# Cross-attention on one core: low parts of the small half by transfer, context scales in one call, once-a-batch steps earlier in VectorE's queue

## The reference

```
xn = layernorm(ctx)            # ctx: 8 x 1601 x 192, gain and bias
ln = layernorm(layernorm(x))   # the latents, 64 a batch
q  = ln @ Wq.T
k, v = split(concat([xn @ Wkv.T, ln @ Wlkv.T], axis=1))
q, k = rmsnorm(q) * gain, rmsnorm(k) * gain        # per head of 64
attn = softmax(where(mask, q @ k.T / sqrt(64), -max))
x = x + (attn @ v) @ Wo.T + bo
```

## Time and profile before

| what | value |
|---|---|
| median of 3 runs | 519.65 us (518.51 to 521.28) |
| the profiled execution's own time | 514.96 us |
| its span, first to last instruction | 513.2 us |
| mean granted TensorE clock | 0.967 |
| TensorE busy | 427.2 us (83%) |
| VectorE busy | 402.1 us (78%) |
| GpSimd busy | 244.7 us (48%) |
| ScalarE busy | 239.1 us (47%) |

### The profile page before, as it was taken

How to read it: one execution, slowest core, us unless ns; L and a number is a source line. 1 busy time by engine, 2 the same in 40 slices (tenths; PEclk the granted TensorE clock), 3 DMA queues, 4 the chain that set the end, 5 groups by cost and what they waited for, 6 DMA issues and landing times.

```text
span 513.2 us, 6607 instructions
## 1 busy us (share of the span) xinstructions
PE 427.2 (83%) x2042; PEld 332.5 (65%) x2042; DVE 402.1 (78%) x969; ACT 239.1 (47%) x547; POOL 244.7 (48%) x248
## 2 busy tenths in 40 slices
PE   3786758788889878978989969887997789789996
PEld 0363535567767766867767758764374667568885
DVE  5846789999999999999988896425569556887776
ACT  0237744556575656755556535321242115335551
POOL 6351866658458465584575542001521331445550
PEclk9998978989999999999999999899999986999999
DMA  8604932040141131403100002910000000000001
GB/s 247 186 1 138 251 129 66 2 142 2 52 142 52 26 119 52 140 4 121 29 3 1 2 0 79 406 40 0 0 2 0 1 0 0 1 1 1 0 2 42
DMA packets 23975, 31.80 MB, mean 62 GB/s; under 512 B 2954, under 2 KB 19652, under 8 KB 23940
## 3 DMA queue, kind: packets, MB, share of 16 engines
q1 hardware_dynamic: 23940, 31.38, 19.8%
HBM read 30.69 MB, written 0.52 MB: 61 GB/s over the span
## 4 chain that ended last, share of the span: by engine, by line
DVE 42%; PE 29%; POOL 15%; issue 10%; ACT 2%; DMA 1%; SPq 1%; DVEq 0%; POOLq 0%; ACTq 0%
PE bank L571 27%; POOL kr L481 10%; DVE kss L1406 6%; DVE arena L1418 5%; DVE arena L1454 5%; DVE split_b L1397 5%; DVE cst L1343 3%; DVE arena L1613 2%; POOL crs L447 2%; DVE arena L1627 1%; DVE kguard L1409 1%; DVE big L1328 1%; DVE cmv L1347 1%; DMA mask_in<-in_p_mask 1%; DVE split_b L1687 1%
## 5 line engine op out<-in xcount | busy, mean ns | idle before, releaser
L571 PE MATMUL bank<-keyq,split_b 128*128 128x512 f32 (+2 forms) x724 | 168.4, 380 | 21.4 <-DVE split_b L1687 7.5
L571 PEld LDWEIGHTS bank<-keyq,split_b 128*128 128x128 f32 (+1 forms) x724 | 123.0, 192 | 52.3 <-issue 19.0
L481 POOL TENSOR_TENSOR kr<-kguard,neg_half 128x8 f32<-128x8 f32 (+1 forms) x56 | 93.3, 1666 | 104.6 <-DVE kguard L1409 104.4
L571 PE MATMUL bank<-arena 128*128 128x193 f32 (+4 forms) x528 | 100.0, 332 | 8.4 <-DVE arena L1613 4.4
L571 PEld LDWEIGHTS bank<-arena 128*128 128x128 f32 (+2 forms) x528 | 85.6, 192 | 18.2 <-issue 13.0
L1130 ACT ACTIVATE arena<-bank 128x512 f32<-128x512 f32 (+1 forms) x56 | 31.6, 563 | 73.4 <-PE bank L571 72.8
L571 PE MATMUL bank<-split_b,keyq 128*128 128x512 f32 x204 | 51.8, 405 | 0.0
L1397 DVE TENSOR_TENSOR split_b<-arena,split_b 32x256 fp32r<-32x256 f32 (+1 forms) x112 | 47.5, 424 | 2.5
L1418 DVE TENSOR_TENSOR arena<-bank,kr 128x512 f32<-128x512 f32 (+1 forms) x56 | 36.0, 643 | 15.3 <-POOL kr L481 15.1
L571 PEld LDWEIGHTS bank<-split_b,keyq 128*128 128x128 f32 x204 | 39.1, 197 | 7.7
L470 POOL TENSOR_TENSOR split_b<-arena,split_b 128x256 fp32r<-128x256 f32 (+1 forms) x56 | 38.4, 685 | 8.9 <-ACT split_b L1105 8.8
(11 more groups left out here) (221 smaller groups left out, 613.5 us busy)
## 6 DMA issues: line engine op xcount, KB each, us to landing
arena<-in_ctx SPq DMA_DIRECT2D x16, 576.0 KB, 4.2
arena<-in_p_ctxT SPq DMA_DIRECT2D x8, 800.5 KB, 6.4
arena<-in_p_ctxT SPq DMA_DIRECT2D x8, 400.2 KB, 7.1
arena<-in_p_experts SPq DMA_DIRECT2D x1, 2688.0 KB, 18.4
arena<-in_p_experts SPq DMA_DIRECT2D x1, 2304.0 KB, 12.1
arena<-in_p_experts SPq DMA_DIRECT2D x1, 1536.0 KB, 6.5
X<-in_x SPq DMA_DIRECT2D x1, 512.0 KB, 3.7
arena<-in_t_Wlkv SPq DMA_DIRECT2D x1, 512.0 KB, 6.9
```

The costliest lines, as they stand in the source:

```text
L481: pool.tensor_tensor(kr[0:r, n % 2, 0:k], kg_[0:r, n % 2, 0:k], neg_half[0:r, 0:4 * k].rearrange("p (t h) -> p t h", h=H), ALU.pow).then_i ...
L571: return nc.tensor.matmul(out_, l, r, start=start, stop=stop, skip_group_check=shared)
```

## The change

It does four things. First, `split_side` goes from VectorE. GpSimd subtracts all 64 small channels in one instruction, as a second part of `split_rest`, into a new tile `side_low` with two slots, and SyncE moves the result to partitions 96 to 127 of `xs` with two transfers of 32 partitions per group (`move_side`). TensorE waits for the transfers in place of the subtraction, and GpSimd, before it writes a slot again, for the transfers out of it. Second, SyncE's loop runs over groups: the moves of group `u + 2` stand first at each step, the loads are placed at steps 0, 1, 2 and 4 of a batch, the mixer's weights go out one a step from step 14 on. Third, GpSimd computes the context scales of a batch in one call with 13 columns at g 2. Fourth, VectorE does `evac_latent_out` ahead of the sums and `refold_low_part` right behind them, and ScalarE copies refolded keys (`twin`) at g 1 in place of g 0. The title of the change also names the scaling of the scores in the step of their sums; `norm_scores(u)` stands in the step of `key_sums(u)` before and after.

```diff
+        side_low = sb("side_low", [SMALL, 2, 256], F32R)
...
+            def move_side(n):
+                k = 256 if n % NG < NG - 1 else TAIL
+                sp.wait_ge(xs_side, n + 1)
+                for j in range(2):
+                    sp.dma_start(xs[n % 3][96:P, 2 + j, 0:k].bitcast(F32), side_low[32 * j:32 * j + 32, n % 2, 0:k].bitcast(F32)).then_inc(side_in[n % 3], 16)
...
+            move_side(0)
+            move_side(1)
+            for u in range(groups):
+                b, g = divmod(u, NG)
+                if u + 2 < groups:
+                    move_side(u + 2)
+                if g == 0 and b + 2 < B:
...
                     load_context(b + 2, 0)
+                if g in (1, 2) and b + 1 < B:
+                    load_turned(b + 1, g - 1)
+                if g == 4 and b + 1 < B:
+                    spread_sd(b + 1)
+                if g == 4 and b + 2 < B:
                     if b + 2 >= 4:
                         sp.wait_ge(y_part, NG * (b - 1))
                     load_context(b + 2, 1)
+                if 2 * NG <= u < 2 * NG + len(mixer_weights):
+                    dst, src = mixer_weights[u - 2 * NG]
+                    sp.dma_start(dst, src).then_inc(mixer_in, 16)
...
-            def context_scales(b, part):
+            def context_scales(b):
+                pool.wait_ge(caggr, 2 * b + 2)
                 k = b % 2
+                then(pool.tensor_scalar(cve[:, k], cmv[:, k, :, 1], LN_EPS, None, ALU.add))
+                then(pool.tensor_tensor(crs[:, k], cve[:, k], neg_half[:, 0:FULL + 1], ALU.pow))
+                if b:
                     pool.wait_ge(sdT_mm, b)
+                pool.tensor_tensor(csd[:], cve[:, k], crs[:, k], ALU.mult).then_inc(ctx_ready, 2)
...
                 pool.tensor_tensor(v[:, 1, 0:k], raw[:, 0], v[:, 0, 0:k].bitcast(F32), ALU.subtract).then_inc(xs_rest, 1)
+                pool.wait_ge(xs_small, n + 1)
+                if n >= 2:
+                    pool.wait_ge(side_in[(n - 2) % 3], 32 * ((n - 2) // 3 + 1))
+                pool.tensor_tensor(side_low[:, n % 2, 0:k], raw[0:SMALL, 1], v[0:SMALL, 2, 0:k].bitcast(F32), ALU.subtract).then_inc(xs_side, 1)
...
                 if g == 2 and b + 1 < B:
-                    context_scales(b + 1, 1)
+                    context_scales(b + 1)
...
-                if g == 0 and b + 1 < B:
-                    context_scales(b + 1, 0)
...
-                pe.wait_ge(xs_side, n + 1)
+                pe.wait_ge(side_in[n % 3], 32 * (n // 3 + 1))
...
+                if g == 1 and 2 <= b <= 5:
+                    act.wait_ge(refold_high, b - 1)
+                    twin((b + 2) % 4 + 1, (b + 2) % 4 + 2)
...
+                if g == 4 and 2 <= b <= B + 1:
+                    evac_latent_out(b - 2)
                 if u < groups:
                     key_sums(u)
+                if g == 0 and 2 <= b <= 5:
+                    refold_low_part(b + 2)
                 if g == 3 and 2 <= b <= B + 1:
                     evac_sum(b - 2)
-                if g == 4 and 2 <= b <= B + 1:
-                    evac_latent_out(b - 2)
...
-                if u + 2 < groups:
-                    split_side(u + 2)
...
-                if g == 0 and 2 <= b <= 5:
-                    refold_low_part(b + 2)
```

More of the change, by code:

```diff
@@ L236, in build @@
         sdT_mm = sem("sdT_mm"); sdT_evac = sem("sdT_evac")
-        sd_rest = sem("sd_rest"); xs_split = sem("xs_split"); xs_rest = sem("xs_rest"); xs_small = sem("xs_small"); xs_side = sem("xs_side")
+        sd_rest = sem("sd_rest"); xs_split = sem("xs_split"); xs_rest = sem("xs_rest"); xs_small = sem("xs_small"); xs_side = sem("xs_side"); side_in = [sem(f"side_in{i}") for i in range(3)]
         k_mm = sem("k_mm"); k_sq = sem("k_sq"); k_ss = sem("k_ss"); k_r = sem("k_r"); s_norm = sem("s_norm"); s_max = sem("s_max")
@@ L349, in _ @@
             sp.wait_ge(pool_const, 1)
-            load_turned(0)
+            mixer_weights = (
+                    (wo[:], a["t_Wo"].rearrange("(c p) n -> p c n", p=P)),
+                    (bo[:], a["L0_xattn_bo"].rearrange("(o d) -> o d", o=1)),
+                    (sums[:], a["c_sums"]), (pick[:], a["c_pick"]), (headsel[:], a["c_head"]),
+                    (wx0[:], a["t_W_x0"].rearrange("(c p) n -> p c n", p=P)),
+                    (wx2b[:], a["t_W_x2"][P:160, :]),
+                    (wr[:], a["t_W_r"].rearrange("(c p) n -> p c n", p=P)),
+                    (wk[:], a["t_W_k"].rearrange("(c p) n -> p c n", p=P)),
+                    (ww1[:], a["t_W_w1"].rearrange("(c p) n -> p c n", p=P)),
+                    (ww2[0:64, :], a["t_W_w2"]), (ww2[64:65, :], a["L0_attn_b_w2"].rearrange("(o d) -> o d", o=1)),
+                    (wv[:], a["t_W_v"].rearrange("(c p) n -> p c n", p=P)),
+                    (wg[:], a["t_W_g"].rearrange("(c p) n -> p c n", p=P)),
+                    (wo2[:], a["t_W_o"].rearrange("(c p) n -> p c n", p=P)),
+                    (gatew[:], a["t_gate_w"].rearrange("(c p) n -> p c n", p=P)),
+                    (ebias[:], a["L0_ffn_e_bias"].rearrange("(o d) -> o d", o=1).broadcast_to([P, NE])),
+                    (before[:], a["c_before"].broadcast_to([P, NE * NE])),
+                    (gbefore[:], a["c_gbefore"].broadcast_to([P, 16])),
+            )
+            for c in range(2):
+                load_turned(0, c)
             load_context(1, 0)
@@ L353, in _ @@
             spread_sd(0)
-            for b in range(B):
-                if b + 2 < B:
+            move_side(0)
[5 more added lines that the diff above has]
+                if g == 0 and b + 2 < B:
                     if b + 2 >= 4:
@@ L438, in rstd @@
                 pool.tensor_tensor(rs[:, lo:hi], rs[:, lo:hi], neg_half[:, 0:hi - lo], ALU.pow).then_inc(ln_rstd, 1)
-            def context_scales(b, part):
-                pool.wait_ge(caggr, 2 * b + part + 1)
+            def context_scales(b):
+                pool.wait_ge(caggr, 2 * b + 2)
                 k = b % 2
-                of = slice(0, 6) if part == 0 else slice(6, FULL + 1)
-                n = of.stop - of.start
-                then(pool.tensor_scalar(cve[:, k, of], cmv[:, k, of, 1], LN_EPS, None, ALU.add))
-                then(pool.tensor_tensor(crs[:, k, of], cve[:, k, of], neg_half[:, 0:n], ALU.pow))
-                if b and part == 0:
+                then(pool.tensor_scalar(cve[:, k], cmv[:, k, :, 1], LN_EPS, None, ALU.add))
+                then(pool.tensor_tensor(crs[:, k], cve[:, k], neg_half[:, 0:FULL + 1], ALU.pow))
+                if b:
                     pool.wait_ge(sdT_mm, b)
-                pool.tensor_tensor(csd[:, of], cve[:, k, of], crs[:, k, of], ALU.mult).then_inc(ctx_ready, 1)
+                pool.tensor_tensor(csd[:], cve[:, k], crs[:, k], ALU.mult).then_inc(ctx_ready, 2)
             def mask_bias():
@@ L1388, in refold_low_part @@
                 last.then_inc(refold_low, 1)
-            def split_side(n):
-                b, g = divmod(n, NG)
-                dve.wait_ge(xs_small, n + 1)
-                k = 256 if g < NG - 1 else TAIL
-                v, side_ = xs[n % 3], ctxT[b % 2][:, 1, 256 * g:256 * g + k]
-                for j in range(2):
-                    last = V.tensor_tensor(v[96:P, 2 + j, 0:k], side_[32 * j:32 * j + 32], v[32 * j:32 * j + 32, 2 + j, 0:k].bitcast(F32), ALU.subtract)
-                last.then_inc(xs_side, 1)
             def key_sums(n):
```

47 lines of the change are left out of this document (9 added, 38 removed).

## The result

| kernel | median, us | runs, us | loop: first to last scaling, us | behind the last scaling, us |
|---|---|---|---|---|
| before, profiled 514.96 | 518.88 | 518.27 to 521.41 (16) | 55.12 to 317.30 | 195.9 |
| changed, profiled 524.92 | 523.69 | 520.89 to 527.30 (16) | 52.07 to 323.77 | 199.3 |

The ratio is 1.0082, 95% interval 1.0057 to 1.0108: slower by 0.8%, 4.8 us, where 532 us (12.35 more than the median shown) was forecast. The two right columns are read from the two profiles: positions of the scaling of the scores in VectorE's timeline, and the span less the last of them.

The account below looks back on a forecast made before the run. VectorE was taken as the bound, but only just. Terms of -1, +11.4, +1, +3 and 0 made +14 us on 514.96, or 529; on the median 533.7, taken as 532, range 512 to 540 us.

Parts of the forecast that it names:

- the sum up to the last scaling: Ahead of the loop -1, batches 0 to 5 +11.4, batch 0 +1 more, batch 6 +3, batch 7 0: +14 us.
- batches 0 and 1: Costed in 6 x (2.6 - 0.7) = +11.4 us for batches 0 to 5, with +1 more in batch 0.
- the gain ahead of the loop: Four subtractions (1.7 us) leave VectorE ahead of the loop; gain 1.0 us, bounds 0 and 1.7.
- the gains at the steps near the floor: Guard to scaling cannot go under GpSimd's 1.91 us for 8 columns; gains 0.45 at step 1, 0.8 at step 6.
- the step from profile to median: The same 14 us on the median 519.65 give 533.7; 532 taken for near ties VectorE may win.
- would show it: Signs: maximum or shift 1.0 to 1.3 us, some 6.5 us to step 2, VectorE idle about 1 us at steps 1, 4, 5.
- meetings: GpSimd's new subtraction overlaps VectorE's two-operand steps, mostly the running maximum: about 0.5 us each, 2.6 us a batch taken.
- The rival without meetings: New subtraction starts before the scaling or gives way to the maximum: faster, 510 to 515 us, chance 0.19.
- The context scales in one call: 13 columns ahead of step 2's power take 3.4 us, GpSimd 6.45 us scale to scale: loss 1.9 us a batch.
- GpSimd bound in every step: Rival: contention makes step 2's 1.9 us 2.9, +8 us, 540; chance 0.13 together with late moves.
- Late moves: Rival: moves 2 us beyond their 3.7 us slack give +16 us, 548; chance 0.13 together with a slower step 2.
- Nothing from the title's scaling: Scaling already stands in the step of its sums and the diff leaves it: no time from it.

Follow-up runs that it names:

- e3: The changed kernel with GpSimd's new subtraction cut to 32 of 256 columns, the transfers as large as before: 505.76 us, 0.9704 of before.
- e6: The changed kernel with the side subtraction back on VectorE and no moves, the rest of the change kept: 519.12 us, 0.9967 of before.
- e15: The changed kernel with three throwaway matmuls in each of TensorE's three short waits behind the loop: 519.86 us, 1.0012 of before.
- the second profile: The kernel before, unchanged, profiled again: 518.41 us (one run) against 514.96 in its first profile.
- e10: The kernel before with only the new order of the once-a-batch steps: 517.25 us, 0.9970 of before.
- e14: The changed kernel with each move cut into two of half the columns, no new wait in SyncE's queue: 524.63 us, 1.0091 of before.
- e13: The changed kernel with VectorE's next key sums and guard ahead of the running maximum, ScalarE's squares in their old place: 491.79 us, 0.9462 of before.
- e16: The kernel before with the new once-a-batch order and early key sums and guard; side subtractions on VectorE, scales in two calls: 510.77 us, 0.9824.

## Why the prediction was right in sign and wrong in size

The step that failed is the sum up to the last scaling: +14 us were added up and +6.5 measured. The terms that were mis-sized are batches 0 and 1, which were costed like batches of the middle, the gain ahead of the loop, and the gains at the steps near the floor; the step from profile to median, scaled up from the profile, failed with it. The mechanism was the one forecast. Of what "would show it", all three came: two-operand steps of 1.15 to 1.23 us, 6.52 us to step 2, and 0.94 us of waiting at steps 4 and 5 (0.47 at step 1). The terms, as means over batches 2 to 5 of the way to each scaling in us. e3 stands for the change without meetings, except at step 2, where it also shortens GpSimd's queue; there the measured change is changed - before, whole:

| way to step | before | e3 | changed | forecast without meetings | measured (e3 - before) | forecast meeting | measured (changed - e3) |
|---|---|---|---|---|---|---|---|
| 0 | 5.08 | 4.98 | 5.44 | 0 | -0.10 | 0.6 | 0.46 |
| 1 | 5.12 | 4.04 | 4.51 | -1.11 | -1.08 | 0.58 | 0.47 |
| 2 | 4.58 | 6.05 | 6.53 | +1.9 | +1.95 | 0.25 | (in it) |
| 3 | 5.41 | 4.41 | 4.88 | -0.9 | -1.00 | 0.5 | 0.46 |
| 4 | 4.53 | 4.87 | 4.87 | +0.55 | +0.34 | 0 | 0 |
| 5 | 4.79 | 4.57 | 4.97 | -0.1 | -0.22 | 0.5 | 0.41 |
| 6 | 4.70 | 3.67 | 4.15 | -0.8 | -1.03 | 0.5 | 0.48 |
| sum | 34.21 | | 35.35 | -0.46 (taken -0.7) | -1.14 | 2.93 (taken 2.6) | 2.28 |

- **The meetings** are real and of the size forecast, 0.41 to 0.48 us each against 0.5 to 0.6: 2.28 us a batch outside step 2, where the same terms add up to 2.68 (2.6 was taken, with step 2). The rival without meetings would have needed less than 0.7.
- **The context scales in one call** were sized right: 6.53 us to step 2, forecast 6.45 and 0.25 for a meeting.
- **The steps at the floor** gained more than costed: step 6 came to 1.28 us from guard to scaling, not 1.5, with a power of 1.00 us for the 65 rows, and the latent output cost 0.34 at step 4, not 0.55. A batch of the middle so lost 1.14 us (35.35 - 34.21) and not 1.9. Against the terms without meetings, five of the seven steps came out 0.1 to 0.25 us better.
- **Ahead of the loop** the mis-sized term is the gain of 1.0 us: it was 3.05, above its own bound of 1.7. e6, with the subtractions back on VectorE, starts its loop at 55.45 us, so they are most of it. VectorE's timeline of the kernel before has the place:

```profile
46.15 2.15 DVE L1397 TENSOR_TENSOR split_b<-arena,split_b 32x256 fp32r<-32x256 f32 x4
```

They hold VectorE's queue for 2.18 us (0.42 of it a meeting: one took 0.84), and the statistics and the first sums behind them come earlier by all of it. The work ahead of them started 0.52 us earlier in the changed kernel's profile, and the other 0.35 us lie in small gaps and waits. The wait for folded queries, for which 0.7 us had been taken off, is TensorE's and took nothing from this.

- **Batch 0** lost 0.9 us and batch 1 0.6, not 2.9 and 1.9. Part of the meetings was not there: the ways to step 1 (3.25 us in batch 0, 3.24 in batch 1) and batch 0's way to step 6 (3.02 us) are as long with the subtraction as without it (e3). In the kernel before they took 4.58, 4.39 and 4.10 us. Batch 6 lost 2.2 (forecast 3); batch 7 lost 1.3 up to its last scaling (forecast 0; TensorE's two waits there fell by 1.25 us, but VectorE's ways to steps 1, 2, 4 and 5 grew by 0.2 to 0.5 us each). Together -3.05 + 6.0 + 2.2 + 1.3 = 6.5 us at the last scaling, where the sum had +14. That is 7.5 of the 8.3 us between 532 and 523.7.
- **The step from profile to median** also failed: "the same 14 us on it give 533.7" took both kernels' ordinary runs to lie equally far above their profiles. 514.96 + 6.5 = 521.4 lies in the lower bunch of the changed kernel (520.9 to 522.7), and 3.4 us of half clock behind the loop, which e15 takes out, give 524.9, its profile. Whether the upper and the lower bunch differ by this stretch stays open (e15). The kernel before lies 3.9 us above its profile for other reasons, of which the second profile and e10 show one.
- **GpSimd bound in every step** did not come (GpSimd sat idle 1.43 us ahead of the power of 130.90). **Late moves** did not come either; e14 shows the slack of the middle, and that batch 0 has less. **Nothing from the title's scaling**: the scores are scaled in the same step of the timeline as before.

The Trainium skill, "SBUF — State Buffer", section "SBUF: two separate sides", has the port pair locked for a whole instruction of the engine that came first. The subtraction rows agree (0.41 to 0.48 us a meeting); the powers do not: the shift at 131.60 took 0.68 us inside the power of 130.90 to 132.54. The measurement decides, and the order of e13 rests on it.

## What to carry to other kernels

Before moving work from a busy engine to an idle one, lay the new instruction on the timeline at the place where the queue will start it, and look at what the other engine does in that very 0.7 us: here the change cost 0.8% with its subtraction beside a two-operand step, and beside a one-input sum it was worth 3.7% (0.9462 against 0.9824). The 3.7% are not the meeting's alone, since the second order also puts the maximum and the shift under the power, and VectorE is then the bound without the change (e16). In the old order, with most of the subtraction left out, the change would have brought 3.0% (e3). Find such an order by asking what the waiting engine needs first (the guard) and putting everything else behind it. Take two profiles before scaling a sum to a median: at an edge of 1%, one 3-us stretch at half clock is as large as the change.

## What the runs showed of the hardware

- The clock granted to TensorE fell to 0.50 (1.2 GHz) behind waits of 0.66 to 0.92 us in the changed kernel's profile (349 to 358 us) and stayed at 1.00 behind the same waits in both profiles of the kernel before; 2.63 us of waiting in the loop gave both outcomes as well. Filling the waits kept it at 1.00 in the stretches shown.
- A meeting costs whichever instruction comes second, GpSimd's too: an addition of 13 columns took 0.69 us instead of 0.26.
- A power is touched by VectorE only at its start. In e13 one that began while a maximum had 0.53 us left took 2.02 us instead of 1.64; the shift that ran later inside it took 0.68 us and lengthened neither. The power of 1.86 us in the earlier trace rows is such a case: a subtraction of the earlier trace rows began 0.05 us ahead of it. The three rows, GpSimd's first:

```profile
154.77 2.02 POOL L499 TENSOR_TENSOR kr<-kguard,neg_half 128x8 f32<-128x8 f32 x1 [0.20 <-DVE kguard L1415]
```

```profile
154.61 0.69 DVE L1439 TENSOR_TENSOR arena<-arena 128x512 f32<-128x512 f32 x1
...
156.09 0.68 DVE L1460 TENSOR_TENSOR arena<-arena,side 128x512 f32<-128x512 f32 x1
```
